# Cross attention scores over 64 rows instead of 32, and another order of work on ScalarE

## The reference, cut

```python
Q = (x_text @ Wq).reshape(Bb, Tt, H, DH)
K = (x_vision @ Wk).reshape(Bb, Gg, H, DH)
scores = jnp.einsum('bthd,bghd->bhtg', Q, K) / np.sqrt(DH).astype(np.float32)
scores = jnp.where(vision_mask[:, None, None, :], scores, -jnp.inf)
topv, topi = jax.lax.top_k(scores, K_TOP)
probs = jax.nn.softmax(topv, axis=-1)
attn = jnp.zeros_like(scores).at[bi, hi, ti, topi].set(probs)
attn_mean = attn.mean(axis=1)
c_t = jnp.einsum('btg,bgd->btd', attn_mean, x_vision @ Wv)
```

## Time and profile before

| | us |
|---|---|
| median of three runs | 5045.92 |
| the profiled execution | 5042.79 |
| its span, first to last instruction | 5040.9 |
| cross stage's loop, tiles 0 to 9 | 978 to 1676 |
| cross stage's loop, tiles 12 to 30 | 1820 to 3312 |
| TensorE matmuls busy | 4416.3 (88%) |
| VectorE busy | 3805.5 (75%) |
| ScalarE busy | 2068.8 (41%) |
| GpSimd busy | 2186.9 (43%) |

### The profile page before, as it was taken

How to read it: one execution, slowest core, us unless ns; L and a number is a source line. 1 busy time by engine, 2 the same in 40 slices (tenths; PEclk the granted TensorE clock), 3 DMA queues, 4 the chain that set the end, 5 groups by cost and what they waited for, 6 DMA issues and landing times. The chain is left out here.

```text
span 5040.9 us, 70529 instructions
## 1 busy us (share of the span) xinstructions
PE 4416.3 (88%) x28066; PEld 3194.9 (63%) x28066; DVE 3805.5 (75%) x4097; ACT 2068.8 (41%) x3816; POOL 2186.9 (43%) x2260
## 2 busy tenths in 40 slices
PE   8999977589999999999999999987579989898984
PEld 6777753356665676676766667667456666666662
DVE  5666659699999988888788887876256767777667
ACT  3433322144444444444444444431234545444453
POOL 1111116435454566766667666670233333333321
PEclk9999988678888877777777777788789999999996
DMA  2111115300011001111011110023531211111101
GB/s 84 51 46 50 49 48 185 118 24 28 24 42 61 26 28 34 38 53 36 28 32 38 54 37 26 30 69 76 193 104 43 61 44 58 47 58 54 51 26 36
DMA packets 214587, 275.98 MB, mean 55 GB/s; under 512 B 96659, under 2 KB 144403, under 8 KB 210224
## 3 DMA queue, kind: packets, MB, share of 16 engines
q1 hardware_dynamic: 196850, 216.91, 14.2%
q0 software_dynamic: 17408, 54.56, 2.9%
HBM read 186.44 MB, written 84.98 MB: 54 GB/s over the span
## 5 line engine op out<-in xcount | busy, mean ns | idle before, releaser
L1555 POOL TENSOR_TENSOR c_s<-c_s,c_z 128x2048 f32<-128x2048 f32 x128 | 580.5, 4535 | 792.8 <-ACT c_z L1344 790.8
L1875 PE MATMUL f_p_g<-f_hT,f_w 128*128 128x128 f32 x4096 | 538.3, 295 | 69.8 <-ACT f_gT L1975 55.4
L1496 DVE MAX8 c_top<-c_z 128x8 f32<-128x2048 f32 x256 | 585.0, 2285 | 4.7 <-issue 0.2
L1875 PEld LDWEIGHTS f_p_g<-f_hT,f_w 128*128 128x128 f32 x4096 | 526.7, 211 | 90.4 <-ACT f_gT L1975 58.2
L1497 DVE MATCH_REPLACE8 c_z<-c_top,c_z 128x2048 f32<-128x2048 f32 x256 | 582.6, 2276 | 0.0
L1169 PE MATMUL c_p_s<-c_kt,c_qT 32*128 32x512 f32 x1024 | 500.9, 864 | 87.1 <-ACT c_s L1334 85.8
L1179 PEld LDWEIGHTS c_p_a<-c_diag,c_s 128*128 128x128 f32 x4096 | 528.2, 211 | 49.5 <-ACT c_diag L1358 25.8
L1179 PE MATMUL c_p_a<-c_diag,c_s 128*128 128x128 f32 x4096 | 531.3, 293 | 25.2 <-ACT c_diag L1358 25.2
L1883 PE MATMUL f_p_o<-f_w,f_gT 128*128 128x512 f32 x1024 | 481.8, 592 | 0.0
L1334 ACT ACTIVATE c_s<-c_p_s 128x512 f32<-128x512 f32 x512 | 278.2, 594 | 455.0 <-PE c_p_s L1170 454.6
L1249 PE MATMUL c_p_m<-c_wf,c_uT 128*128 128x512 f32 x768 | 415.7, 684 | 22.6 <-ACT c_yb L1398 16.3
(11 more groups left out here) (362 smaller groups left out, 8103.4 us busy)
## 6 DMA issues: line engine op xcount, KB each, us to landing
mod_out<-c_fo POOLq DMA_DIRECT2D x32, 512.0 KB, 3.0
f_mr<-mod_out SPq DMA_DIRECT2D x32, 512.0 KB, 4.8
p_ct<-in_ctxT SPq DMA_DIRECT2D x16, 768.0 KB, 5.1
c_vals<-in_ctx SPq DMA_DIRECT2D x4, 3072.0 KB, 12.0
c_kb<-kspec SPq DMA_DIRECT2D x22, 512.0 KB, 3.3
a_xt<-in_xT SPq DMA_DIRECT2D x32, 256.0 KB, 3.1
a_xr<-in_x SPq DMA_DIRECT2D x32, 256.0 KB, 2.6
x<-a_out POOLq DMA_DIRECT2D x32, 256.0 KB, 2.5
```

The costliest lines, as they stand in the source:

```text
L1496: st.link(v.max(best[n], work))
L1555: pool.tensor_tensor(row, row, low, ALU.subtract).then_inc(cut_ready, 1)
L1875: last = mm(p_g[:, f % 8, :], w1[:, k, f * P:(f + 1) * P], hT[:, k * P:(k + 1) * P], start=(k == 0 and f % 4 == 0), stop=(k == KD - 1 and ...
```

## The change

Each head's queries are kept with the other head of its half zeroed: `qT[:, 0]` holds heads 0 and 2, `qT[:, 1]` heads 1 and 3, made by two copies with a scale per partition from a new tile `hm` of ones and zeros. A matmul takes 64 rows of it against 64 rows of the keys, so a pair is now one head of the lower half (rows 0 to 63) and one of the upper (rows 64 to 127): the zeroed head adds nothing. `qT` is no longer double by tile. The mask's row is loaded at partitions 0 and 64 only, two DMAs a batch instead of four. On ScalarE, `copy_s` for both parts now stands ahead of `weigh` and `diagonal`, and `below(j + 2)` ahead of `copy_slot`.

```diff
-                for h in range(NH2):
-                    sp.dma_start(mrow[HS * h:HS * h + 1, :], mask_row[b:b + 1, :]).then_inc(keys_in, 16)
+                for r in (0, 2 * HS):
+                    sp.dma_start(mrow[r:r + 1, :], mask_row[b:b + 1, :]).then_inc(keys_in, 16)
...
-                pe.wait_ge(keys_in, 80 * (t // CH + 1))
+                pe.wait_ge(keys_in, 48 * (t // CH + 1))
                 for c in range(4):
                     cols = slice(c * 512, (c + 1) * 512)
                     for i in range(2):
-                        r = HS * (2 * p + i)
+                        r = 2 * HS * i
                         at_least(pe, s_copied, (t * 2 + p) * 8 + 2 * c + i - 1)
-                        mm(p_s[:, i, :], qT[r:r + HS, t % 2, :], kt[r:r + HS, cols], start=True, stop=False)
+                        mm(p_s[:, i, :], qT[r:r + 2 * HS, p, :], kt[r:r + 2 * HS, cols], start=True, stop=False)
                         mm(p_s[:, i, :], oneb[r:r + 1, :], mrow[r:r + 1, cols], start=False, stop=True).then_inc(s_done, 1)
...
-                a(qT[:, t % 2, :], p_m[:, 1, 0:P], ACT.Copy).then_inc(q_copied, 1)
+                for p in range(2):
+                    last = a(qT[:, p, :], p_m[:, 1, 0:P], ACT.Copy, scale=hm[:, p:p + 1])
+                last.then_inc(q_copied, 1)
...
+            act.wait_ge(hm_ready, 2 * NH2)
             copy_q(0)
...
                 copy_s(t, 1, 0)
+                copy_s(t, 1, 1)
                 if t:
                     weigh(j - 1)
                     diagonal(j - 1)
-                copy_s(t, 1, 1)
                 if t + 1 < TILES:
                     copy_q(t + 1)
...
                 if t + 1 < TILES:
                     copy_s(t + 1, 0, 0)
+                    copy_s(t + 1, 0, 1)
                 weigh(j + 1)
                 diagonal(j + 1)
-                if t + 1 < TILES:
-                    copy_s(t + 1, 0, 1)
+
+                below(j + 2)
                 if slot_job(t) is not None:
                     copy_slot(t)
-
-                below(j + 2)
...
+            for h in range(NH2):
+                v.memset(hm[HS * h:HS * h + HS, h % 2:h % 2 + 1], 1.0).then_inc(hm_ready, 1)
+                v.memset(hm[HS * h:HS * h + HS, 1 - h % 2:2 - h % 2], 0.0).then_inc(hm_ready, 1)
             dve.wait_ge(core_in, 16 * 3)
```

More of the change, by code:

```diff
@@ L918, in cross @@
         tb = m.sb("tb", [P, 2])
+        hm = m.sb("hm", [P, 2])
         den = m.sb("den", [P, 2])
@@ L963, in cross @@
         p_m = m.ps("p_m", [P, 2, 512])
-        (core_in, film_in, consts, keys_in, values_in, s_done, s_copied, z_done, nb_ready, tb_ready, low_ready, cut_ready,
+        (core_in, film_in, consts, hm_ready, keys_in, values_in, s_done, s_copied, z_done, nb_ready, tb_ready, low_ready, cut_ready,
          sum_done, rd_ready, w_ready, im_ready, diag_ready, attn_done, aT_copied, uT_done, uT_copied,
@@ L971, in cross @@
             m.sem(n) for n in (
-                "core_in film_in consts keys_in values_in s_done s_copied z_done nb_ready tb_ready low_ready cut_ready "
+                "core_in film_in consts hm_ready keys_in values_in s_done s_copied z_done nb_ready tb_ready low_ready cut_ready "
                 "sum_done rd_ready w_ready im_ready diag_ready attn_done aT_copied uT_done uT_copied "
```

## The result

| | us, median | range | ratio to before (95%) |
|---|---|---|---|
| before | 5047.09 (4 runs) | 5042.34 to 5048.26 | 1 |
| after | 5509.24 (4 runs) | 5506.64 to 5513.35 | 1.0918 (1.0899 to 1.0937) |

A forecast was written before the change was run, and what follows sets the result against it. It took TensorE's loop as the bound, busy 1398 of 1492 us. Added were +314 (late tiles), +133 (tiles 1 to 7), +44 (8 to 10), +16 (ends): +507 on 5042.8, 5550 us; likeliest case 5400 to 5620, eight in ten 4940 to 5600.

The forecast's parts named there:

- heads in sequence and the clock falling: Likeliest case for TensorE's scores: two heads run one after another and the clock drops; 5550 us, chance 0.50.
- the fast rival: Scores' two heads still overlap and the clock stays at 2.4 GHz; about 4945 us, chance 0.28.
- Heads in sequence: In the scores, the second head waits for the first head's mask matmul; a two-head chunk takes 2.88 us, before 2.03.
- The price of a head: One head's scores and mask in a chunk on TensorE: 1.44 us at 2.4 GHz, 2.65 at 1.2.
- the second gap: Idle time on TensorE at the size change after a head's mask matmul: 0.10 us at 2.4 GHz.
- 0.05 for the load of the mask's weights: Uncovered half of the 0.09 us mask weight load, counted in each head's time at 2.4 GHz.
- the first gap: Idle time on TensorE at the size change between a head's scores and its mask matmul: 0.10 us at 2.4 GHz.
- The clock: TensorE's clock in the scores falls to 1.2 GHz about 5 us into a pair, making it 17.2 us.
- The case for a kept clock: Rival: scores' heads in sequence but TensorE, busy without pause, keeps full clock; 5170 us, chance 0.14.
- The sum: Whole-kernel total: +314 us late tiles, +133 tiles 1 to 7, +44 tiles 8 to 10, +16 first tile and last pair.
- The rival of order alone: Scores' heads overlap and the clock falls, so only ScalarE's order counts; 5110 us, chance 0.06.
- VectorE's waits for `c_rd` gone behind the slot but new ones elsewhere: Profile sign: VectorE's 10.5 us wait behind the slot transform disappears while other waits appear.

The follow-up runs named there:

- e1: The changed kernel with the mask's matmul also over 64 rows, zeros in all but the mask's row; 4895.7 us, ratio 0.9698 to before.
- e4: The kernel before with only the mask's matmul widened to 64 rows, scores still over 32 and the old order; 5422.6 us, ratio 1.0740.
- e5: The changed kernel with every scores and mask matmul over all 128 rows, heads one after another; 4944.7 us, ratio 0.9797 to before.
- e3: The kernel before with only ScalarE's new order, scores still over 32 rows; 5102.9 us, ratio 1.0102.
- e2: The changed kernel with ScalarE's old order put back, scores over 64 rows kept; 5428.7 us, ratio 1.0753 to before.
- e6: e1 with the queries' transposes copied ahead of weigh and diagonal, and the slot's result ahead of below(j+2); 4783.0 us, ratio 0.9476 to before.

## Why the prediction was right

Forecast were 5550 us (5400 to 5620 for this case); measured were 5509.2. The step on which all hung, heads in sequence and the clock falling, was given 0.50, and e1 shows that the 0.28 of the fast rival was no empty chance: with one line altered its steps came true to 0.1 us. Its time was 50 us off (4945 forecast, 4900 to 4980, and 4895.7 measured): a late tile lost 7.0 us and not 5.3, and the early ones cost nothing where 1.1 each were forecast.

**Heads in sequence.** Right. The row that carried it was the load that waited for the streams to end. e1 and e4 show it from both sides. The Trainium skill, TensorEngine Tiling (Array Packing), Key Properties, says that a change of tiling mode drains TensorE. The gaps of some 0.1 us in the changed kernel and in e4, and the overlap that e1 has without them, agree.

**The price of a head.** 1.44 us forecast, 1.37 measured; at the lower clock 2.65 and 2.54. Two rows of the weight loads show the passage:

```profile
2534.76 0.29 PEld L1170 LDWEIGHTS c_p_s<-c_kt,c_qT 64*128 64x128 f32 x2
2535.81 0.09 PEld L1171 LDWEIGHTS c_p_s<-c_mrow,c_oneb 1*128 1x128 bf16 x1 [0.76 <-issue]
2536.13 0.29 PEld L1170 LDWEIGHTS c_p_s<-c_kt,c_qT 64*128 64x128 f32 x2 [0.23 <-issue]
```

The head's load and two streams end at 2534.76 + 0.11 + 0.86 = 2535.73, and the mask's load begins 0.08 later. From there to the next head's load it is 0.32 us, of which the mask's stream is 0.22; the remaining 0.10 holds either the mask's own load or the second gap, not both. The term "0.05 for the load of the mask's weights" was thus too much, as was 0.02 of the first gap: 0.07 a head, 0.6 us a pair at the high clock and somewhat more at the low.

**The clock.** Right in kind and place: it fell 5.5 us into the pair from 2534.76 and 3.8 us into the one from 2488.66 (forecast some 5). The case for a kept clock was answered with a row read wrongly: the 1.83 of 2 us busy stand in a stretch that already ran at 0.50, where the same work takes longer. At 1.00, in the first pair's second chunk, TensorE was busy 1.48. The choice was right, that support for it was not. Part of the price can be told apart by the sequence that keeps the clock. e5's pair is 8 x 1.075 = 8.6 us. With the changes of size, but at 2.4 GHz, it would be 8 x 1.37 = 11.0; measured are 15.6 to 17.0. So against e5 the changes of size cost 2.4 us a pair directly, and 4.6 to 6.0 us came with the lower clock. Against the kernel before it is an even split: its pairs of 10.2 us ran partly at the lower clock too, and e1's overlapping pairs at the full one take 7.95. By that estimate about half of the 6 us that a pair took longer, 3.0, are the sequence and its gaps, and the other half is more time at the lower clock.

**The sum.** A pair took 16.4 us on average, not 17.2. At 1.37 and 2.54 us a head that is 3.4 heads ahead of the fall, just what was forecast (1.7 chunks), so the mis-sized term is the price of a head: 3.4 x 0.07 + 4.6 x 0.11 = 0.7 of the 0.8 us. Over the late tiles film starts 23.5 to 24.6 us after the scores, 24.0 on average (25.1 forecast), and queries 19.4 to 20.4, on average 20.0 (20.75). Against the earlier trace rows that is +6.0 and +7.9, 13.9 and not 15.7 us, and with 20 tiles it is nearly the whole miss: 20 x 1.8 = 36 of 41 us. The early tiles, with 18.3 us for each against 19, and the three without a slot were right within some 5 us.

**Where the order counts.** The forecast let VectorE gain nothing from the reorder, and `below` cost only where nothing covers it. e3 agrees in sum: late tiles unchanged, early ones 46.8 us longer. In its late tiles the two steps did move as forecast: film came 17.4 or 18.1 us after the scores (18.04 before), the queries' second step 13.6 to 13.8 (12.07). The forecast missed that the rest of the tile gave it back: from the queries' second step to the next pair it was 25.5 or 27.5 us where it had been 28.0, and in the shorter of these the granted clock was 0.93 in place of 0.84. The rival of order alone was 5110 us against 5102.9 in e3, but by two misses that cancel: +26 forecast for the late tiles and 0 measured, +36 and +47 for the early.

**The forecast for the profile.** "VectorE's waits for `c_rd` gone behind the slot but new ones elsewhere" was the one weak sentence: the sum rose to 406.6 us. The longest is 15.5 us where it was 10.6. It changed nothing in the time, for the reason given there: nobody waits for VectorE.

**Left open.** Why the two parts together cost 23 to 29 us more than the sum of each alone was not separated. By the starts of the copies it stands in the late tiles: there the order costs 34.0 us when sizes change in turn (e2 against the changed kernel) and 2.9 when they don't (e3), in the early ones 36.1 and 46.8. Nor was a kernel run with a change of size and the clock kept up, so the split of 2.4 and 4.6 to 6.0 us rests on arithmetic from e5's rows and not on a run of its own.

## What to carry to other kernels

Before you widen or narrow one matmul, look at the one issued next to it. A mask matmul of 64 rows beside scores of 32 cost this kernel 377 us without a single added column, and zeros that bring the small matmul up to its neighbour's size gave the changed kernel 614 us back (the mask's matmul took 0.38 us with 1 row and with 128). And when a stage of TensorE runs at half clock though it is busy, try more of its rows; with that done, look for the waits of 2 us and more in it, since here the work behind them often ran at the lower clock too.

## What the runs showed of the hardware

- Two heads of 64 rows run side by side as two of 32 do: four f32 matmuls of 512 columns with their loads in 1.13 us in both (the earlier trace rows and e1).
- With 1 row beside 64 (after) and 64 beside 32 (e4) a matmul waits for the streams in front of it; in the first its rows lie apart from the next head's. With 1 beside 32 and 65 beside 128 it doesn't. The gap is 0.08 to 0.10 us, small beside the lost overlap (2.74 us a chunk for 2.03) and the clock.
- TensorE at work with 64 and 1 rows in turn fell to 1.2 GHz in 3.6 to 5.5 us in each of 60 pairs. With 128 rows (e5) it stayed at 2.4 for the whole pair in 58 of 60, with 64 and 64 in 59 (e1) and 56 (e6), with 32 and 1 (before) in none.
- A wait can cost more than its length. Behind 2.76 us of waiting eight matmuls took 2.08 us (1.60 a tile later), behind 0.69 us they took 1.16. In e6 that came on top of the waits themselves.
